# Attention windows: POOL builds the score mask from VectorE's selection, between its gathers

## What is computed

```python
e = (e_attr @ We + be).reshape(-1, H, C)
ke = k[src] + e
alpha = (q[dst] * ke).sum(-1) / jnp.sqrt(jnp.asarray(C, x.dtype))
amax = jax.ops.segment_max(alpha, dst, num_segments=n)
ex = jnp.exp(alpha - amax[dst])
den = jax.ops.segment_sum(ex, dst, num_segments=n)
w = ex / (den[dst] + 1e-16)
msg = (v[src] + e) * w[:, :, None]
out = jax.ops.segment_sum(msg.reshape(-1, H * C), dst, num_segments=n)
```

## Time and profile before

| | us |
|---|---|
| three runs: median (lowest to highest) | 4366.57 (4356.75 to 4371.01) |
| the profiled execution | 4329.4 |
| its span, first to last instruction | 4327.6 |
| mean granted clock of TensorE | 0.916 |

### The profile page before, as it was taken

One profiled execution on the slowest core, in us unless ns is written; L12 is line 12 of the kernel. 1 busy time (PEld: TensorE's weight loads), 2 busy tenths in 40 slices (PEclk: granted clock), 3 DMA queues, 4 the chain that ended last, 5 costly groups with the idle time before them and its releaser, 6 DMA issues. The chain is left out here.

```text
span 4327.6 us, 82914 instructions
## 1 busy us (share of the span) xinstructions
PE 3495.6 (81%) x22381; PEld 2067.5 (48%) x22381; DVE 1823.4 (42%) x5369; ACT 1433.0 (33%) x3483; POOL 1862.8 (43%) x1907
## 2 busy tenths in 40 slices
PE   4999999947758888876777777667777769999998
PEld 2666666635534444443444444334443444555564
DVE  4666666647523333332333333323333323344222
ACT  3555555522623333332233323222222223122112
POOL 2555555500256665653566656456666630000000
PEclk8999999979879999998888998878898889999999
DMA  5677775656444554555666666556666645443223
GB/s 139 187 200 199 198 196 167 165 115 204 140 136 137 140 136 131 139 137 136 169 176 172 176 175 179 156 155 167 167 164 168 166 111 176 171 177 118 74 97 125
DMA packets 716528, 675.29 MB, mean 156 GB/s; under 512 B 382359, under 2 KB 542945, under 8 KB 716117
## 3 DMA queue, kind: packets, MB, share of 16 engines
q1 hardware_dynamic: 622598, 466.26, 37.1%
q0 software_dynamic: 77008, 200.24, 17.2%
q10 hardware_dynamic: 16768, 6.91, 0.6%
HBM read 530.84 MB, written 142.28 MB: 156 GB/s over the span
## 5 line engine op out<-in xcount | busy, mean ns | idle before, releaser
L2293 POOL DMA_INDIRECT l_y<-s_lrows,l_src x1344 | 1352.6, 1006 | 964.3 <-issue 352.4
L2373 PE MATMUL ps<-l_y,aw_pT 128*63 128x277 f32 x2700 | 436.8, 467 | 259.9 <-ACT aw_pT L2591 249.1
L3404 PE MATMUL ps<-nl_adj,nl_table 126*128 126x504 bf16 (+1 forms) x3150 | 631.4, 357 | 2.3 <-DVE nl_table L3639 2.3
L998 POOL DMA_INDIRECT em_gs<-s_rows,em_idx x400 | 432.3, 1081 | 325.8 <-DVE em_a L1189 147.9
L2357 PE MATMUL ps<-aw_yT,aw_qt 128*63 128x384 f32 x1800 | 377.2, 529 | 120.0 <-DMA aw_yT<-s_dxT 61.2
L3404 PEld LDWEIGHTS ps<-nl_adj,nl_table 126*128 126x128 bf16 x3150 | 301.8, 96 | 299.0 <-issue 5.3
L2750 DVE COPY aw_axd<-ps 128x252 f32<-128x252 f32 x225 | 94.7, 421 | 796.9 <-remote 409.9
L2330 PE MATMUL ps<-ident,l_y 128*128 128x128 f32 x1800 | 281.5, 292 | 150.9 <-issue 83.1
L2373 PEld LDWEIGHTS ps<-l_y,aw_pT 128*63 128x63 f32 x2700 | 195.7, 154 | 431.9 <-ACT aw_pT L2591 279.6
L2591 ACT ACTIVATE aw_pT<-ps 128x381 f32<-128x381 f32 x225 | 109.9, 488 | 736.8 <-remote 506.0
L2577 ACT ACTIVATE aw_yT<-ps 128x512 f32<-128x512 f32 (+1 forms) x525 | 261.4, 536 | 245.2 <-remote 114.7
(11 more groups left out here) (381 smaller groups left out, 5866.1 us busy)
## 6 DMA issues: line engine op xcount, KB each, us to landing
nl_adj<-s_adj SPq DMA_DIRECT2D x20, 3100.8 KB
aw_yT<-s_dxT SPq DMA_DIRECT2D x150, 384.0 KB
aw_geoS<-s_geoS SPq DMA_DIRECT2D x450, 94.5 KB
nl_adj<-s_adj SPq DMA_DIRECT2D x15, 2325.6 KB
ws_msg<-s_msg SPq DMA_DIRECT2D x75, 384.0 KB, 3.8
s_dxT<-aw_yT SPq DMA_DIRECT2D x75, 384.0 KB
aw_qt<-s_qt SPq DMA_DIRECT2D x225, 126.0 KB
s_msg<-em_msg SPq DMA_DIRECT2D x100, 256.0 KB
```

Source lines behind the costliest of these rows:

```text
L998: pool.indirect_dma_start(out=gs[:, u, j, :], out_offset=None, in_=d["rows0"], in_offset=bass.IndirectOffsetOnAxis(ap=slot[:, u, 2 * j:2 * ...
L2293: pool.indirect_dma_start(out=y[:, u, j, 0:W], out_offset=None, in_=table, in_offset=bass.IndirectOffsetOnAxis(ap=src[:, u, j:j + 1], axis ...
L2373: m = nc.tensor.matmul(k.ps[64 * v:64 * v + HW, SUM, 0:SW], pT[:, SLOT[u], j, 64 * v:64 * v + HW], y[:, u, v * TH + j, 0:SW], start=j == 0 ...
L3404: m = nc.tensor.matmul(k.ps[:, bank(i, p), 0:cols * WN], source[:, p, q, b, :], adj[:, a % 2, 0:cols, b * WN:(b + 1) * WN], start=b == 0 a ...
```

## The change

`off` is no longer written by DVE in one instruction of 378 columns but by POOL in six of 63, one for each tile. While POOL gathers group w it puts behind each gather of tile j the mask of tile j of group w-2. For that it waits once, at tile 0, for DVE's selection of group w-2; the two waits ahead of tiles 2 and 4 are gone. The last two groups of a layer get their masks behind the loop. DVE keeps the comparison, now called `select`, and does it for the group three ahead (of the first three before the sweep); from the sixth group on it waits for POOL's mask of the group that last used the buffer. PE waits for `masked` ahead of L2348, and in layers 1 and 2 its `sums` also waits for the weighed rows. The semaphores of the query weights (`query_mixed`) are merged with those of the other weights (`mixed`), with other counts.

```diff
@@ -2138,7 +2138,7 @@
         part = sb("part", [GK, 3, WC * V, H, HN], BF16)
         rows = sb("rows", [CW // 2, 2, D])
         xs = sb("xs", [D, CW])
-        w2_in, query_mixed, query_mixed_c = sem("w2_in"), sem("query_mixed"), sem("query_mixed_c")
+        w2_in = sem("w2_in")
         rows_out, qt_out, qs_out, next_src = sem("rows_out"), sem("qt_out"), sem("qs_out"), sem("next_src")
         queried = steps("queried", ["LR", "QK0", "QK1", "QK2", "GEO0", "GEO1"], 2, NWC)
         query_ok = steps("query_ok", ["LR"] + [f"{n}{h}" for h in range(H) for n in "KE"] + [f"G{h}" for h in range(H)], 2, NWC)
@@ -2165,7 +2165,9 @@
     pT_ok = steps("pT_ok", ["P"], U, NW)
     exped = steps("exped", ["E"], U, NW)
     agr_ok = steps("agr_ok", ["AG"], U, NW)
-    ready = steps("ready", ["DX", "SEL", "OFF"], U, NW)
+    ready = steps("ready", ["DX"], U, NW)
+    selected = steps("selected", ["SEL"], U, NW)
+    masked = steps("masked", ["OFF"], U, NW)
     soft = steps("soft", ["MAX", "NEG", "DEN", "INV"], U, NW)
     parts_ok = steps("parts_ok", ["AXD", "AG"], U, NW)
     out_ok = steps("out_ok", ["OWN", "SUM", "X"] + (["XS"] if l < 2 else []), 2, NWC)
@@ -2276,6 +2278,15 @@
         sp.wait_ge(qs_out, 16 * PAIRS * (NWC + 1))
 
     def gpsimd(pool):
+        def mask(w, u, j):
+            if j == 0:
+                pool.wait_ge(selected.sem, selected.of(w, "SEL"))
+                pool.sem_inc(hop["pool"], 1)
+            m = nc.gpsimd.tensor_scalar(off[:, u, j:j + 1, :, :], bc(sel[:, u, j:j + 1, :].unsqueeze(2), [128, 1, H, HN]),
+                                        -1.0, None, ALU.add)
+            if j == T - 1:
+                m.then_inc(masked.sem, 1)
+
         def gather(w, u):
             if started(w, U):
                 pool.wait_ge(summed.sem, summed.of(w - U, "AG"))
@@ -2284,24 +2295,24 @@
                 pool.wait_ge(indexed.sem, indexed.of(w, "SRC"))
                 pool.sem_inc(hop["pool"], 1)
             for j in range(T):
-                if started(w, U) and j == 2:
-                    pool.wait_ge(scored.sem, scored.of(w - 3, "S"))
-                    pool.sem_inc(hop["pool"], 1)
-                if started(w, U) and j == 4:
-                    pool.wait_ge(turned.sem, turned.of(w - 2, "T1"))
-                    pool.sem_inc(hop["pool"], 1)
                 pool.indirect_dma_start(out=y[:, u, j, 0:W], out_offset=None, in_=table,
                                         in_offset=bass.IndirectOffsetOnAxis(ap=src[:, u, j:j + 1], axis=0)
                                         ).then_inc(rows_in[u], 16)
+                if started(w, 2):
+                    mask(w - 2, (u - 2) % U, j)
 
         if before is not None:
             before.src_ready(pool)
             before.rows_stored(pool)
+        masked.prime(pool)
         for u in range(1 if before is None else 0, U):
             gather(u, u)
         with pool.Fori(1, NW // U) as i:
             for u in range(U):
                 gather(U * i + u, u)
+        for u in (U - 2, U - 1):
+            for j in range(0, T, 1):
+                mask(NW - U + u, u, j)
 
     def tensor(pe):
         def mix():
@@ -2341,7 +2352,7 @@
             for v in range(V):
                 nc.tensor.matmul(rows_(v), qs[:, u, v, :],
                                  geoS[:, u, v * HS:(v + 1) * HS].rearrange("f (p j) -> f j p", j=TH), start=True, stop=False)
-            pe.wait_ge(ready.sem, ready.of(w, "OFF"))
+            pe.wait_ge(masked.sem, masked.of(w, "OFF"))
             for j in range(TH):
                 for v in range(V):
 
@@ -2368,6 +2379,8 @@
         def sums(w, u):
             pe.wait_ge(pT_ok.sem, pT_ok.of(w, "P"))
             pe.wait_ge(agr_ok.sem, agr_ok.of(w - 1, "AG"))
+            if l:
+                pe.wait_ge(ready.sem, ready.of(w, "DX"))
             for j in range(TH):
                 for v in range(V):
                     m = nc.tensor.matmul(k.ps[64 * v:64 * v + HW, SUM, 0:SW], pT[:, SLOT[u], j, 64 * v:64 * v + HW],
@@ -2715,14 +2728,12 @@
             nc.vector.tensor_tensor(y[:, u, :, D:2 * D], y[:, u, :, W - D:W], bc(y[:, u, :, G0:G0 + 1], [128, T, D]),
                                     ALU.mult).then_inc(ready.sem, 1)
 
-        def mask(w, u):
-            s = ready.sem
+        def select(w, u):
+            if started(w, U):
+                dve.wait_ge(masked.sem, masked.of(w - U, "OFF"))
             nc.vector.tensor_tensor(sel[:, u, :, :], bc(k.iota_wn[:, 0:HN].unsqueeze(1), [128, T, HN]),
                                     bc(k.dl[:, bass.ds(w, 1), :].rearrange("p w t -> p (w t)").unsqueeze(2), [128, T, HN]),
-                                    ALU.is_equal).then_inc(s, 1)
-            dve.wait_ge(s, ready.of(w, "SEL"))
-            nc.vector.tensor_scalar(off[:, u, :, :, :], bc(sel[:, u, :, :].unsqueeze(2), [128, T, H, HN]), -1.0, None,
-                                    ALU.add).then_inc(s, 1)
+                                    ALU.is_equal).then_inc(selected.sem, 1)
 
         def maximum(w, u):
             s = soft.sem
@@ -2806,7 +2817,8 @@
                 indices(w + U - 1, (u - 1) % U)
             if not (isinstance(w, int) and w == NW - 1):
                 weigh(w + 1, (u + 1) % U, i if u < U - 1 else i + 1)
-                mask(w + 1, (u + 1) % U)
+            if not (isinstance(w, int) and w + 3 >= NW):
+                select(w + 3, (u + 3) % U)
             if started(w, 1):
                 denominator(w - 1, (u - 1) % U)
             maximum(w, u)
@@ -2827,7 +2839,7 @@
         if before is not None:
             before.tensor_done(dve)
             before.scalar_done(dve)
-        for s in (ready, soft, indexed, parts_ok, out_ok) + ((geo_ok,) if queries else (joined_ok,)):
+        for s in (ready, selected, soft, indexed, parts_ok, out_ok) + ((geo_ok,) if queries else (joined_ok,)):
             s.prime(dve)
         if before is None:
             dve.sem_inc(indexed.sem, 1)
@@ -2838,7 +2850,8 @@
         else:
             dve.sem_inc(indexed.sem, U)
         weigh(0, 0, 0)
-        mask(0, 0)
+        for u in range(3):
+            select(u, u)
         sweep(dve, turn)
         c = NWC - 1
         denominator(NW - 1, U - 1)
...
-                m.then_inc(query_mixed, 1)
+                m.then_inc(mixed, 1)
             elif n == 1:
-                pe.wait_ge(query_mixed_c, 2)
+                pe.wait_ge(mixed_c, steps + 2)
...
```

More of the change, by code:

```diff
@@ L2467, in mix_queries @@
                                          start=True, stop=True)
-                m.then_inc(query_mixed, 1)
+                m.then_inc(mixed, 1)
             elif n == 1:
-                pe.wait_ge(query_mixed_c, 2)
+                pe.wait_ge(mixed_c, steps + 2)
                 for h in range(2):
                     m = nc.tensor.matmul(k.ps[:, 6 + h, 0:2 * D + GK], wqT[:, h * D:(h + 1) * D], kb[:, h, :], start=True, stop=True)
-                m.then_inc(query_mixed, 1)
+                m.then_inc(mixed, 1)
             else:
-                pe.wait_ge(query_mixed_c, 4)
+                pe.wait_ge(mixed_c, steps + 4)
                 nc.tensor.matmul(k.ps[:, 6, 0:2 * D + GK], wqT[:, 2 * D:3 * D], kb[:, 2, :], start=True, stop=True)
@@ L2513, in turn @@
                 if queries:
-                    pe.wait_ge(query_mixed_c, 7)
+                    pe.wait_ge(mixed_c, steps + 7)
                 pe.wait_ge(mixed_c, steps)
@@ L2770, in mix_queries @@
         def mix_queries(n):
-            dve.wait_ge(query_mixed, n + 1)
+            dve.wait_ge(mixed, n + 2)
             if n == 0:
-                nc.vector.tensor_copy(wqT[:, :], k.ps[:, 6, 0:H * D]).then_inc(query_mixed_c, 1)
+                nc.vector.tensor_copy(wqT[:, :], k.ps[:, 6, 0:H * D]).then_inc(mixed_c, 1)
                 nc.vector.tensor_copy(kb[:, :, D:2 * D + GK], k.ps[:, 7, 0:H * (D + GK)].rearrange("p (h f) -> p h f", h=H)
-                                      ).then_inc(query_mixed_c, 1)
+                                      ).then_inc(mixed_c, 1)
             elif n == 1:
                 for h in range(2):
-                    nc.vector.tensor_copy(abc[:, h, :], k.ps[:, 6 + h, 0:2 * D + GK]).then_inc(query_mixed_c, 1)
+                    nc.vector.tensor_copy(abc[:, h, :], k.ps[:, 6 + h, 0:2 * D + GK]).then_inc(mixed_c, 1)
             else:
-                nc.vector.tensor_copy(abc[:, 2, :], k.ps[:, 6, 0:2 * D + GK]).then_inc(query_mixed_c, 1)
+                nc.vector.tensor_copy(abc[:, 2, :], k.ps[:, 6, 0:2 * D + GK]).then_inc(mixed_c, 1)
                 bias_of = k.ps[:, 7, 0:3 * H].rearrange("p (h t) -> p h t", t=3)
-                nc.vector.tensor_copy(ab[:, :, 0:2], bias_of[:, :, 0:2]).then_inc(query_mixed_c, 1)
-                nc.vector.tensor_copy(ab[0:GK, :, 2:3], bias_of[0:GK, :, 2:3]).then_inc(query_mixed_c, 1)
+                nc.vector.tensor_copy(ab[:, :, 0:2], bias_of[:, :, 0:2]).then_inc(mixed_c, 1)
+                nc.vector.tensor_copy(ab[0:GK, :, 2:3], bias_of[0:GK, :, 2:3]).then_inc(mixed_c, 1)
```

## The result

| | before | after |
|---|---|---|
| median of four runs (lowest to highest), us | 4368.79 (4356.75 to 4371.52) | 4525.34 (4517.85 to 4531.71) |
| the profiled execution, its span, us | 4329.4, 4327.6 | 4517.85, 4516.0 |
| mean granted clock | 0.916 | 0.897 |

The ratio is 1.0364 (95% interval 1.0345 to 1.0384): 157 us slower by the medians, 188 by the profiled spans. The forecast was 45 us slower. Its sign holds, its size doesn't.

What follows compares the result with a forecast made beforehand. Groups were taken to wait for SP's chain of issues. The terms 0 + 37 + 10 + 3 = +50, less 5 for the shorter DVE chain, put +45 on the median 4366.57: 4411 us, 1.0% slower, range 4300 to 4580.

Steps and rivals of the forecast that it cites:

- What bounds the kernel: In attention a group waits for SP's chain of issues, 5.47 us in layer 2, not for POOL's or DVE's arithmetic.
- DVE, 0: Taking 225 masks of 277 ns off DVE only lengthens its idle: 0, lower bound -62 us.
- POOL, the pair of 1.47 us and 9.6 us a group: Gather 0.95, mask 0.22, gap 0.30; POOL needs 9.6 us a group against periods of 10.3, 10.1 and 9.7.
- The masks' stretch: POOL regains up to 0.28 us a group, its masks wait out DVE's multiply; the sum stays the same within 15 us.
- Masks on the path, +37: PE asks 1 us early in a third of 225 groups, half of these covered: +37 us, bounds 0 and +225.
- The waits removed, +10: Gathers in SP's loads: +25 us in layers 0 and 1, -15 in layer 2, so +10; bounds -128 and +128.
- Layer starts, +3: Mask 0 comes behind the gathers of the first three groups: +1 us a layer, +3; bounds 0 and +10.
- A: POOL's mask fits in the gap and the pace stays 1.25 to 1.35: 4322, faster by 1%; chance 0.30.
- C: PE's 3 us of waiting cover every late mask, gathers only change places in SP's stretch: 4367; chance 0.18.
- B: Pair of 1.88 us, 11.6 us a group, POOL the bound in each layer: +350, 4717; chance 0.14.
- its variant with the gap gone: Pair of 1.58 us, 9.8 us a group, only layer 2 bound by POOL; the forecast grows to 4430.
- The signs: Profile: gathers 1.47 us apart, POOL over 90% busy or in gaps, PE's mask wait 30 to 60, SP's loads stretched.

Runs made afterwards that it cites:

- The shadow run: Changed kernel with POOL's instructions cut to 8 elements in a copy nobody reads, DVE making PE's mask: 4087.86, 4085.63 and 4090.66 us on the second kind.

## Why the prediction was wrong

**What bounds the kernel.** In accord with the traces of the chip it was read on: groups paced by late releases and SP's chain, POOL with slack. It holds on that kind of chip alone; on the other the same program is bound by POOL's stream of gathers.

**DVE, 0.** Right: with the mask doubled instead of removed, the ratio is 1.0000.

**POOL, the pair of 1.47 us and 9.6 us a group.** This is the step that failed. One term was mis-sized, the mask, and with it the conclusion that POOL stays under the period: its own time is 10.3 to 10.4 us a group, not 9.6, against 10.3, 10.1 and 9.7. The mask is 0.42 us where it is undisturbed and 0.466 in the mean, not 0.22: 628 us in all instead of 1350 x 0.22 = 297. I had the row of a COPY of 8 elements below and a select of 128 elements at 325 ns above, and took the value near the COPY because its element count was nearer. The measured value lies above even the upper row: a select of 128 elements doesn't bound an add of 63 with a repeated operand. The shadow run shows that a like instruction of 8 elements takes 0.26 and the 55 more take 0.16. The other parts of the group nearly cancel: the gather behind a mask is 1.03 + 0.17 instead of 0.95 + 0.30, the start of 0.41 that I added doesn't show in the totals, and the gathers total 1445 us against the 6.45 x 225 = 1451 of my sum.

**The masks' stretch.** I wrote that the two rules of the Trainium skill would leave the sum the same within 15 us. They don't: with masks among what is held up, the multiply costs some 0.3 us a group on masks and 0.3 on gathers (0.466 and 1.075 against 0.415 and 1.03, times six). The part of the gathers was in my sum (0.34), that of the masks, some 70 us in all, was not. Cutting the multiply gave back 79 us in two layers, its own shorter time included.

**Masks on the path, +37.** The comparison was the right one, when the last mask is ready against when PE asks, but it treats POOL as if it began each group fresh. With 6 x 1.64 = 9.8 and 0.6 of stretch a group of POOL is above every period of before, and the waits for the sums and the selection (0.5) make it 10.9; there is no slack to be late in, and PE waits 562 us for masks, in 168 groups. Much of that stands in the place of waits that were there before, as the 3.02 us ahead of the sums in the earlier trace rows. What was to be added up is POOL's group and not single waits. By such a sum POOL's own 10.3 to 10.4 us against the mean period of 10.05 give an estimated 55 to 80 us, and the rest of the 188 is what the late masks and sums add, which was not measured by itself on the first kind. On the second kind lateness measures 108 to 125 us of 648.

**The waits removed, +10.** The sign is not confirmed. SP's loads got shorter, from 3.5, 3.9 and 4.7 to 2.8 or 2.9 us by layer, with 1.5 to 1.7 gathers started in them (2.0 to 2.6 before). Restoring the waits moved the ratio from 1.036 to 1.040. What my sum lacked is that the late releases vanish with the change. The changed kernel's groups are equally long on both kinds of chip, while the kernel before pays for late releases on the first; so 648 us of loss show as 157 there.

**Layer starts, +3.** Small, as forecast: by the starts of the groups in the traces, layer 0 begins 4.4 us later than before, and the steps from one layer to the next are 1.4 and 0.1 us longer.

**Rivals.** A (the mask fits in the gap) and C (no change) are out. B had the right mechanism, POOL as the bound in each layer, with too high a price: 1.88 us a pair and 4717, since it took 0.41 for the gather's start and 0.30 for the gap. Between B's 11.6 us a group and my 9.6 the chip gives about 11. Nearest was its variant with the gap gone, a pair of 1.58; but I let that bind layer 2 alone, where it bound all three.

**The signs.** Two of those named came: POOL is busy or in its gaps for some 95% of the three layers, and DVE's maximum is idle for 786 us against 396.9. The others didn't: the pair is 1.64 us, PE's wait ahead of the mask 562 us instead of 30 to 60, SP's loads shorter, and POOL's group over the 10.5 that I had named as a sign of being wrong. The sign of the result was forecast by +37 for late masks and +10 for SP's loads. The first is in the loss, larger and as a consequence of POOL's pace, the second isn't seen, and POOL's pace itself, on which the rest hangs, stood in the sum at nothing; so the right sign is in part luck.

## What to carry to other kernels

Before work is put on an engine that looks half idle, add up that engine's own group: instructions, gaps between them, and stretches, against the period. If the sum reaches the period, the change costs the whole excess, however well the single waits seem covered. The price of an instruction not in the trace should come from a size and a kind like its own; where only unlike rows exist, take the dearer one, or measure it. Idle time that an engine shows on one chip may not be there on another, so a change that spends it can cost four times as much there, as 648 us against 157 here.

## What the runs showed that I had not expected

- The same program takes 4370 us on some chips and 3765 on others, in every run there, with gathers of the same length (1006 and 1001 ns). On the first kind PE's semaphores rise some 2.6 us late in the mean, and they do so while POOL issues gathers; on the second 0.03.
- With a mask behind each gather, in three kernels on the first kind, the delay falls to 0.1 to 0.4 us.
- An add on POOL costs 0.24 us to start and 2.5 to 2.8 ns an element (0.26, 0.42 and 1.19 us for 8, 63 and 378).
- Two rows of POOL depend on what precedes them: a gather behind a gather 0.95 with a gap of 0.30, behind a tensor instruction 1.03 with 0.17. A semaphore increment between two gathers leaves them at 0.95 and 0.30.
- A tensor instruction of 8 elements behind each gather, which nobody reads, cost 8.5% of the whole kernel on the second kind; it adds 0.23 us to each of 1350 gathers of an engine that is the bound.
